# The in_proj of a state-space block as three products of rounded parts, with its weights in a ring

## The reference

```
xn = layernorm(x);  proj = xn @ in_proj_w            # 512 -> 2 x 1024
hidden, gate = split(proj)
hs = silu(conv1d(hidden, conv_w) + conv_b)           # 4 taps, causal
dt, B, C = split(hs @ x_proj_w)                      # each rms-normed
dt = softplus(dt @ dt_proj_w + dt_proj_b)
s_t = exp(dt_t * A) * s_{t-1} + dt_t * hs_t * B_t    # 16 states per channel
y = (sum over states of s * C + hs * D) * silu(gate)
x = x + y @ out_proj_w
```

## Time and profile before

| | |
|---|---|
| three runs | 5323.81, 5326.52, 5327.91 us; median 5326.52 |
| profiled execution | 5325.68 us, its span 5323.8 us |
| PE busy | 4817.2 us, 90% |
| DVE busy | 4447.0 us, 84% |
| GpSimd busy | 3155.8 us, 59% |
| ACT busy | 2689.8 us, 51% |
| granted PE clock, mean | 0.969 |
| DMA | 394.68 MB, 74 GB/s in the mean |

### The profile page before, as it was taken

The page is one execution under the profiler, slowest core; times in us unless marked ns, Lnnn a source line. Parts: engine busy times, 40 slices in busy tenths (PEclk is TensorE's granted clock), DMA queues, the critical chain, the costliest instruction groups (busy, mean ns, idle before and its releaser), DMA issues. The chain is left out here.

```text
span 5323.8 us, 108656 instructions
## 1 busy us (share of the span) xinstructions
PE 4817.2 (90%) x44199; PEld 2788.8 (52%) x44199; DVE 4447.0 (84%) x7289; ACT 2689.8 (51%) x4364; POOL 3155.8 (59%) x1639
## 2 busy tenths in 40 slices
PE   6899999999999999999999999987499999999973
PEld 3344444444444444444444444433388888888862
DVE  3989889898998989889898898985578888888876
ACT  3666666666666666666566665652133333333320
POOL 1676776767767676676766767675144443444436
PEclk9999999999999999999999999998699999999995
DMA  2222212222222222222222222221300000000003
GB/s 86 84 92 85 97 72 104 94 82 104 73 104 89 88 102 75 97 89 87 101 82 96 86 90 102 75 96 64 129 26 28 26 28 26 28 28 26 28 22 78
DMA packets 117198, 394.68 MB, mean 74 GB/s; under 512 B 26720, under 2 KB 28384, under 8 KB 83808
## 3 DMA queue, kind: packets, MB, share of 16 engines
q1 hardware_dynamic: 107040, 383.95, 20.5%
q0 software_dynamic: 6336, 0.18, 0.3%
q10 hardware_dynamic: 3328, 3.61, 0.2%
HBM read 348.20 MB, written 39.50 MB: 73 GB/s over the span
## 5 line engine op out<-in xcount | busy, mean ns | idle before, releaser
L336 POOL TENSOR_TENSOR s<-s,Cb 128x1024 f32<-128x1024 f32 x1024 | 2394.1, 2359 | 996.2 <-DVE state L654 991.9
L649 DVE TENSOR_TENSOR_SCAN s<-s,state,BU 128x512 f32<-128x512 f32 x2048 | 2453.2, 1260 | 368.2 <-PE BU L738 347.7
L505 ACT ACTIVATE s<-dt,ch 128x512 f32<-128x512 f32 x2048 | 1307.0, 715 | 718.9 <-PE Y L755 717.4
L755 PE MATMUL Y<-s,ident 64*64 64x512 f32 x8192 | 1010.4, 609 | 67.0 <-POOL s L336 66.7
L681 PE MATMUL PJ<-xnT,w_in 128*128 128x512 f32 x2048 | 947.0, 606 | 30.1 <-ACT xnT L372 15.3
L738 PEld LDWEIGHTS BU<-spread,dtuT 32*128 32x128 f32 x16384 | 512.3, 189 | 529.7 <-DVE s L649 338.3
L738 PE MATMUL BU<-spread,dtuT 32*128 32x128 f32 x16384 | 609.9, 286 | 146.4 <-DVE s L649 145.7
L681 PEld LDWEIGHTS PJ<-xnT,w_in 128*128 128x128 f32 x2048 | 369.9, 190 | 502.7 <-issue 423.8
L755 PEld LDWEIGHTS Y<-s,ident 64*64 64x64 f32 x8192 | 277.6, 134 | 563.6 <-issue 527.7
L729 PE MATMUL PJ<-w_out,u 128*128 128x512 f32 x1024 | 471.3, 604 | 7.9 <-ACT xnT L372 6.4
L1105 POOL TENSOR_TENSOR x1t<-x1t,bias_b 128x512 f32<-128x512 f32 x64 | 83.0, 1296 | 398.9 <-DVE xa L1291 398.9
(11 more groups left out here) (223 smaller groups left out, 6951.4 us busy)
## 6 DMA issues: line engine op xcount, KB each, us to landing
Cb<-bc SPq DMA_DIRECT2D x256, 1024.0 KB, 4.8
res<-in_x SPq DMA_DIRECT2D x64, 256.0 KB, 5.0
x<-res SPq DMA_DIRECT2D x64, 256.0 KB, 5.1
x1t<-x SPq DMA_DIRECT2D x64, 256.0 KB, 2.6
out<-r_t SPq DMA_DIRECT2D x64, 256.0 KB, 2.0
xt<-in_x SPq DMA_DIRECT2D x31, 512.0 KB, 5.7
rows_of<-out SPq DMA_DIRECT2D x10, 512.0 KB, 7.5
out<-rows_of SPq DMA_DIRECT2D x10, 512.0 KB, 3.6
```

The lines of the kernel that those rows point to most:

```text
L336: nc.gpsimd.tensor_tensor(pair, pair, Cb[q % 2][:, 2 * part * T:2 * part * T + 2 * T], ALU.mult).then_inc(z_ready, 1)
L505: nc.scalar.activation(s[k % SLOTS][:, n, :], dt[p % 2][:, gi, :], ACT.Exp, scale=ch[:, 2 * p + gi, 7 + 4 * nq + n:8 + 4 * nq + n]).then_i ...
L649: nc.vector.tensor_tensor_scan(s[k % SLOTS][:, n, :], s[k % SLOTS][:, n, :], BU[:, n::4], state[:, b, k, n:n + 1], ALU.mult, ALU.add).then ...
L755: last_ = nc.tensor.matmul(Y[r][y_rows(r, gi), :], ident[rows, rows], s[(k_even + gi) % SLOTS][rows, n, :], start=False, stop=(n == 3 and ...
```

## The change

It has these parts:

- in_proj is computed from rounded parts in the type float32r: weight = high + low, x = high + low. Each group is three products of four matmuls: high x high, low x high, high x low; the third waits (in group 0 of a period) for the low part of x.
- The turned x is copied twice by ACT, to `x_high` (rounded) and `x_full` (fp32, room for two blocks); DVE subtracts them to `x_low`, 256 tokens at a time, in its pieces of units 8 and 12.
- The weights no longer fit whole. At the start SP loads them into the four slots s, ACT rounds each of 16 groups, GpSimd subtracts, and SP saves both parts to DRAM (512 KB a group, one behind the other). In the periods a ring of five groups is refilled by GpSimd's own DMAs, one for each group used, issued behind its multiplies in the unit after the use, five groups ahead.
- In unit 12 PE turns x before the sums, and ACT takes x right behind the exponentials of the next unit, ahead of the softplus and the silu; the same place holds for the x of unit 7.
- In the start-up list two gates come before x_proj, DVE doesn't wait for ACT's constants before its layernorm, and the constants of the skip product are made between other copies. SP's reload of x waits for the turn and no longer for the copy.
- Some semaphores are shared or renamed.

```diff
-        w_in = sb("w_in", [P, KB, 2 * INTER])
+        w_ring = sb("w_ring", [P, RING, 2, KB, P], F32R)
...
-        xnT = sb("xnT", [P, KB, T])
+        x_high = sb("x_high", [P, KB, T], F32R)
+        x_low = sb("x_low", [P, KB, T], F32R)
+        x_full = sb("x_full", [P, KB, 2 * P])
...
+            def save_w(n):
+                held(w_low_ready, n + 1)
+                held(w_saved, 16 * n)
+                sp.dma_start(w_split[n], slot_of(n).bitcast(F32)).then_inc(w_saved, 16)
...
             load_x(ahead, ("xT", 1), 0, 0, 0, 1)
+            for n in range(NG - 2):
+                save_w(n)
             store_bc(ahead, 0, 0)
             sp.wait_ge(bc_stored, 16)
             load_c(0, 0)
+            for n in range(NG - 2, NG):
+                save_w(n)
...
+            def low_w(n):
+                wait(pool, w_high_ready, n + 1)
+                nc.gpsimd.tensor_tensor(w_ring[:, n % RING, 1], w_raw[n // 4][:, :, n % 4, :], w_ring[:, n % RING, 0],
+                                        ALU.subtract).then_inc(w_low_ready, 1)
...
+            def refill(ring_, use, period, n):
+                wait(pool, ring_.full, ring_.filled(use, period))
+                m = n + RING
...
+                wait(pool, w_refilled[m % RING], refills(m) - 16)
+                nc.gpsimd.dma_start(slot_of(m), w_split[m % NG]).then_inc(w_refilled[m % RING], 16)
...
+                    if k - 1 in GATE_AT:
+                        m = GATE_AT[k - 1]
+                        n = NG * (c if m >= 6 else c + 1) + G + m
+                        if n + RING < NG * NCH:
+                            refill(steady, ("gate", m), c, n)
+                    if k - 1 in HID_AT:
+                        n = NG * (c + 1) + HID_AT[k - 1]
+                        if n + RING < NG * NCH:
+                            refill(steady, ("hid", HID_AT[k - 1]), c, n)
...
+            def high_w(n):
+                if n % G == 0:
+                    act.wait_ge(w_raw_loaded[n // G], 16 * (2 * KB + n // G * 3))
+                if n >= RING:
+                    act.wait_ge(w_saved, 16 * (n - RING + 1))
+                nc.scalar.copy(w_ring[:, n % RING, 0], w_raw[n // 4][:, :, n % 4, :]).then_inc(w_high_ready, 1)
...
-                nc.scalar.copy(xnT[:, :, j * P:(j + 1) * P],
-                               PJ[ring_.bank(("xT", j))][:].rearrange("p (k t) -> p k t", k=KB)
-                               ).then_inc(ring_.taken["act"], 1)
-
+                bank = PJ[ring_.bank(("xT", j))][:].rearrange("p (k t) -> p k t", k=KB)
+                nc.scalar.copy(x_high[:, :, j * P:(j + 1) * P], bank)
+                if j == 2:
+                    wait(act, x_low_ready, 2 * c_next + 1)
+                nc.scalar.copy(x_full[:, :, j % 2 * P:(j % 2 + 1) * P], bank).then_inc(ring_.taken["act"], 1)
...
-                    if k in XT_AT:
-                        for j in XT_AT[k]:
-                            if last:
-                                act.drain().then_inc(steady.taken["act"], 1)
-                            else:
-                                take_x(steady, j, c)
...
+                    if first and k < SLOTS:
+                        act.wait_ge(w_low_ready, NG // SLOTS * (k + 1))
                     for n in range(4):
                         nc.scalar.activation(s[k % SLOTS][:, n, :], dt[p % 2][:, gi, :], ACT.Exp,
                                              scale=ch[:, 2 * p + gi, 7 + 4 * nq + n:8 + 4 * nq + n]).then_inc(da_ready, 1)
+                    if k - 1 in XT_AT:
+                        for j in XT_AT[k - 1]:
+                            if last:
+                                act.drain().then_inc(steady.taken["act"], 1)
+                            else:
+                                take_x(steady, j, c, c + 1)
                     long_piece(k - 1)
...
+            def low_x(ring_, period, c_next, half):
+                dve.wait_ge(*ring_.emptied(("xT", 2 * half + 1), period))
+                cols = slice(2 * half * P, 2 * half * P + 2 * P)
+                nc.vector.tensor_tensor(x_low[:, :, cols], x_full[:], x_high[:, :, cols], ALU.subtract
+                                        ).then_inc(x_low_ready, 1)
...
+                        if k in (8, 12):
+                            low_x(steady, c, c + 1, 0 if k == 8 else 1)
...
+                if n < NG:
+                    wait(pe, w_low_ready, n + 1)
+                else:
+                    wait(pe, w_refilled[n % RING], refills(n))
+                w_high, w_low = w_ring[:, n % RING, 0], w_ring[:, n % RING, 1]
                 for kb in range(KB):
-                    last_ = nc.tensor.matmul(bank[:], w_in[:, kb, lo:lo + P], xnT[:, kb, :],
-                                             start=(kb == 0), stop=(kb == KB - 1))
+                    nc.tensor.matmul(bank[:], w_high[:, kb, :], x_high[:, kb, :], start=(kb == 0), stop=False)
+                for kb in range(KB):
+                    nc.tensor.matmul(bank[:], w_low[:, kb, :], x_high[:, kb, :], start=False, stop=False)
+                if n % NG == 0:
+                    wait(pe, x_low_ready, 2 * (n // NG) + 2)
+                for kb in range(KB):
+                    last_ = nc.tensor.matmul(bank[:], w_high[:, kb, :], x_low[:, kb, :],
+                                             start=False, stop=(kb == KB - 1))
                 last_.then_inc(ring_.full, 1)
...
-                    if k == 12:
-                        sums(k)
                     main(k)
-                    if not sums_first and k != 12:
+                    if not sums_first:
                         sums(k)
```

More of the change, by code:

```diff
@@ L159, in mamba_block @@
         two = (0, 1)
-        ahead = ring(uses("xT", 0, 1, 2, 3) + uses("hid", *range(G)) + uses("xp", *two) + uses("turn", *two)
-                     + uses("dt0", *two) + uses("gate", 0, 1, 2, 3) + uses("tr0", *two) + uses("gate", 4, 5), "ahead")
+        ahead = ring(uses("xT", 0, 1, 2, 3) + uses("hid", *range(G)) + uses("gate", 0, 1) + uses("xp", *two)
+                     + uses("turn", *two) + uses("dt0", *two) + uses("gate", 2, 3) + uses("tr0", *two)
+                     + uses("gate", 4, 5), "ahead")
         steady = ring(uses("dt1", *two) + uses("out", 0) + uses("gate", 6, 7) + uses("out", 1) + uses("tr1", *two)
@@ L186, in y_rows, with refills, slot_of @@
             return slice(at, at + 64)
+        def refills(n):
+            return 16 * sum(1 for q in range(NG, n + 1) if q % RING == n % RING)
+        def slot_of(n):
+            return w_ring[:, n % RING].rearrange("p h k n -> p (h k n)")
         def block_of(ap, tb):
@@ L320, in _ @@
                 spread_b(0, nq)
+            for n in range(NG - 2, NG):
+                low_w(n)
+            def refill(ring_, use, period, n):
+                wait(pool, ring_.full, ring_.filled(use, period))
+                m = n + RING
+                if m < 2 * NG:
+                    wait(pool, w_saved, 16 * (m - NG + 1))
+                if m - RING < NG:
+                    wait(pool, w_saved, 16 * (m - RING + 1))
+                wait(pool, w_refilled[m % RING], refills(m) - 16)
+                nc.gpsimd.dma_start(slot_of(m), w_split[m % NG]).then_inc(w_refilled[m % RING], 16)
+            for m in range(3, 6):
+                refill(ahead, ("gate", m), 0, G + m)
             def body(i, b, c, first, last):
@@ L340, in body @@
                         spread_b(c, 3)
+                    if k - 1 in GATE_AT:
[7 more added lines that the diff above has]
+                            refill(steady, ("hid", HID_AT[k - 1]), c, n)
+                    if k == 0 and not first:
+                        n = NG * c + G + GATE_AT[U - 1]
+                        if n + RING < NG * NCH:
+                            refill(steady, ("gate", GATE_AT[U - 1]), c - 1, n)
                     if k in (28, 29, 30) and not last:
@@ L439, in _ @@
             dt_exp_log()
-            for m in range(4):
-                take_gate(ahead, m, 0)
+            take_gate(ahead, 2, 0)
+            high_w(G + RING + 2)
+            take_gate(ahead, 3, 0)
             take_dtu(ahead, 0, 0)
@@ L607, in _ @@
                 ln_apply(0, half)
+            for half in range(2):
+                low_x(ahead, 0, 0, half)
+            dve.wait_ge(consts_ready, 1)
             for m in range(G):
@@ L764, in _ @@
             pe.wait_ge(ahead.taken["act"], NT)
-            pe.wait_ge(w_hid_loaded, 16 * KB)
             for m in range(G):
-                project(ahead, ("hid", m), 0, m * P)
-            pe.wait_ge(w_loaded, 16 * (KB + 3))
+                project(ahead, ("hid", m), 0, m)
+            for m in range(2):
+                project(ahead, ("gate", m), 0, G + m)
+            pe.wait_ge(w_raw_loaded[1], 16 * (2 * KB + 3))
             for tb in range(TB):
```

108 lines of the change are left out of this document (62 added, 46 removed).

## The result

| | before | after |
|---|---|---|
| median of runs | 5326.1 us (5323.81 to 5327.91, 4 runs) | 5371.32 us (5368.06 to 5379.17, 4 runs) |
| profiled execution / its span | 5325.68 / 5323.8 us | 5369.12 / 5367.3 us |
| first unit's BU product | 114.22 | 108.87 |
| last unit's BU product | 3677.04 | 3716.77 |

The ratio is 1.0088, 95% interval 1.0075 to 1.0101: slower by 45 us, where I forecast 25 (5351, its own range 5334 to 5388).

A forecast was written before the change was run, and what follows sets the result against it. PE and DVE were both near the bound, deciding unit by unit. Per period -1.77 + 0.53 + 2.63 + 1.17 = +2.56 us, 15 times +38.4, start -13: 5325.7 + 25.4 = 5351, own range 5334 to 5388, chance 0.50.

The forecast's parts named there:

- Part 1: In_proj groups: 12 matmuls take 2.90 us instead of 3.63; 1.77 us a period gained in units 20, 26/27, 30 and 31.
- Part 2, unit 8: Output group in unit 8 waits for one more ACT copy of x: 0.53 us a period lost.
- Part 2, unit 12: DVE's subtraction behind unit 12's scans waits for all four ACT copies; unit 14's scans start late: 2.63 us a period lost.
- doesn't bring this forward: Unit 12: PE's new order does not make x's copies earlier; x is turned by 1320.6, its bank waiting until 1319.95.
- Part 3: Ring refills by GpSimd, 1.84 us each: no room in units 27 to 31, unit 30's sums late, 1.17 us a period lost.
- Rival C: Refills held by DVE operations with two SBUF inputs: +7.0 us a period, 5418; chance 0.10, though called the outcome by the skill's rule.
- The about 1 us before the first byte: Skill's figure for a GpSimd DMA; used instead of 1.84 for a refill, the 1.17 loss would be gone.
- Part 4: Start: 16.5 us gained, including 9.9 behind L717, less 3.5 for saves, C's load and subtractions: 13 won; bounds 0 and 16.5.
- The 2.6 booked for ACT's constants: Start: DVE no longer waits for ACT's constants, so the first in_proj group comes at about 31 instead of 33.84.
- The sum: A period costs +2.56 us, 15 periods +38.4; with the start's -13, +25.4 on 5325.7 gives 5351.
- lower edge: Low end of the forecast's own range, 5334, from refills at 0 and the start at -16.5.
- What was named as a sign: 12 matmuls in 2.9, PE near 0.90, periods 226.5, DVE idle 3.5 in unit 12, GpSimd DMAs 1 to 2, first unit near 100.

The follow-up runs named there:

- Run 1: Kernel before, only each in_proj group made 12 matmuls on rounded tiles; no low parts, ring, refills, x_low or second copy: 5291.15 against 5324.54, ratio 0.9937.
- run 2: Changed kernel, x_low's second half subtracted behind the scans of unit 13 instead of unit 12: 5349.27, ratio 1.0041 to the kernel before.
- run 4: Changed kernel without the ring's refills and the waits for them, so later periods use stale weights: 5371.72, ratio 1.009 to the kernel before.
- run 12: Kernel of run 11, with four refills put off to units 1, 5, 6 and 7 of the next period: 5314.02 against 5326.60, ratio 0.9973.
- run 7: Changed kernel, GpSimd's subtractions for weight tiles 0 and 1 ahead of the power for x's second half: one execution, 5361.56.
- run 3: Changed kernel, ACT copies each turned block to x_full first, gives the bank back, then rounds both blocks from x_full: 5349.88, ratio 1.0047 to the kernel before.
- run 6: Changed kernel with 8 matmuls of zeros added to Y on PE in unit 8: 5374.92, ratio 1.0088 to the kernel before.
- run 11: Changed kernel with the changes of run 2, run 3, run 5, run 7, group 0's third product in unit 14, zero matmuls in unit 28: 5320.81, ratio 0.9989.
- run 10: As run 11 without zero matmuls, but DVE's reduction of unit 27 ahead of the ssm normalisation: 5388.85, ratio 1.0115 to the kernel before.
- Run 8: Changed kernel with high parts in all three products, low parts computed but never multiplied: 5368.82, ratio 1.0085 to the kernel before.
- run 5: Kernel of run 2, with PE's sums of unit 12 ahead of the turn of x again: 5345.42, ratio 1.0033 to the kernel before.

## Why the prediction was right, and where it wasn't

- **Part 1** (-1.77 a period): right. Run 1 has -1.85, with units 26, 27, 30 and 31 at 6.84, 6.09, 6.09 and 7.38, and unit 28 at 6.90 instead of 6.09, which gives most of what 26 and 27 won back, as the forecast had it. Its total was 5291 where 5290 was expected.
- **Part 2, unit 8** (+0.53): the size was right, 0.49 in the short kind. What the step left out is that the clock can fall with PE's longer idle time, 1.7 more each time.
- **Part 2, unit 12** (DVE waits for all four copies, +2.63): right in kind and size. The wait is 3.36, units 12 to 22 lost 2.4 with the 0.25 of unit 20 already in it (in run 1 the same units gained 0.33, so the wait's own price is 2.8). But one sentence was incomplete: that PE's new order "doesn't bring this forward" is true, and it also costs 0.8 of its own, hidden behind DVE's wait. That is why run 2, which took the wait away, gave 0.8 and not 2.2: PE's late BU product of unit 13 and its third product came next.
- **Part 3** (+1.17, refills at 1.84): over-priced, by the nearest row, an indirect DMA. A direct one took 0.58 on GpSimd (0.53 to 0.79) and landed in 4.8; the refills cost 0.4 a period in unit 31, not in the sums of unit 30, and in some periods up to 0.9 in unit 4, where they make C's load late, a cost that the forecast put at nothing; runs 4 and 12 show both. Rival C did not come: beside the convolutions no row of L366 is over 0.79. The prediction's "by that rule C is the outcome" didn't follow: what the Trainium skill says of descriptors (SBUF — State Buffer, SBUF: two separate sides) is said of DVE's two-port modes, and of L548 the prediction knew only its two SBUF inputs. The about 1 us before the first byte (the Trainium skill, DMA: Bandwidth & Descriptors, Latency and other measured facts) can't be read off these rows, which time the issue and the landing.
- **Part 4** (-13): mis-sized, -5.35. Three things failed. In_proj began at 35.70, not 31, and of this GpSimd's subtractions in the way of DVE's normalisation are 1.9 (run 7: 33.83, no earlier than before). The 2.6 booked for ACT's constants were not there: DVE's statistics of the second half began at 26.83, released by the load of x, where they began at 27.46 before, and PE then waits 1.29 for ACT's copies instead of 0.68. And DVE's three L636 of a convolution took 3.27 instead of 2.40 while the subtractions ran, so x_proj began at 73.26, where it began at 70.65 before. From there on 8.0 us were won (35.6 from x_proj to the first unit instead of 43.6), where 9.9 were expected.
- **The sum.** The short kind costs +1.86 a period where I said +2.56, so without the long periods the change would have stood near 5326 - 5 + 28 = 5349, beside the forecast of 5351. That this agrees is luck in part: too high a price for the refills (some 12 us in 15 periods) and too large a gain in the start (8 us) cancelled. Most of the 20 us by which the run was over the forecast, some 17, is the term I did not have: falls of PE's granted clock. The prediction's own lower edge was a little off as well: refills at 0 and a start of -16.5 give 5330, not 5334.
- **What was named as a sign**: groups of 12 matmuls in 2.9, PE at 0.904, DVE's wait of 3.4, all as said; periods of 225.5 where 226.5 was named. The GpSimd rows of 1 to 2 us and the first unit near 100 were not.

That the falls need PE's idle time is shown where it was taken away (runs 3 and 6 at unit 8, run 11 at unit 28) and by the count over all 14 profiles, periods 1 to 14. At unit 8 the clock fell in 20 of 84 periods in the six kernels in which PE idles 0.95 there, and in none of 112 in the eight in which it idles 0.46 or is filled. At unit 28 it fell in 39 of 140 where PE idles 1.0 and 1.5, in none of 42 where it idles 1.3 once or 0.5, and in 14 of 14 where it idles 5.3 (run 10). So the idle time is needed, and one or two microseconds of it do not suffice: that a given stretch brings a fall in one period and not in the next is seen and not explained. Run 8 excludes the values of the low parts, run 4 the refills. Runs 1 and 5 have the idle stretches of unit 28 and no fall there. What else decides stays open, as does the further 3.8 us behind the last unit (in the profiles here the time from the last unit to the end was between 1645.8 and 1650.6).

## What to carry to other kernels

When a change relieves PE without moving the other bound, price PE's new idle stretches as well: here an idle microsecond ahead of a burst of matmuls cost up to 1.7 more, in a quarter of the cases. Before a wait is removed, list who is late next with times; a wait that is over only a little earlier is hidden behind it, and here one removal gave a third of its price. Where DVE and GpSimd hold each other up, look at which one is idle now because of a late release: here releasing GpSimd earlier cost 64 us. And a transfer that is cheap to issue can still make another one late, as the refills did with C.

## What the runs showed that I had not expected

- A granted clock of 0.50 inside a stretch in which PE is 90% busy, after idle stretches of 1 to 2 us, and 4 to 8 matmuls at about one and a half times their time or more (5.37 instead of 3.67; 2.05 instead of 1.20).
- Matmuls of zeros in such a gap keep it at 1.00, and pay if they fit in the gap (two of 1.09 in unit 28), not if they are longer (1.95 in 0.95).
- A 512 KB transfer costs GpSimd 0.58 us and is cheap to place, but four of them in a full stretch cost 0.4 us a period and made C's load late, for up to 0.9 more.
- DVE's 64-column operations at 2.3 us each beside GpSimd's multiplies.
